# First cross-attention of a two-layer decoder: K and Q projected as three fp32r products of split weights and inputs, and the last unit's division and output projection taken in quarters

## The reference

```python
# x: (4, 512, 256), ctx: (4, 1024, 256), 16 heads of 64
q = x @ Wq; k = ctx @ Wk; v = ctx @ Wv          # fp32, 256 -> 1024 channels
p = softmax(mask(q @ k.T * 0.125))              # a context row that is all zero is masked
x = layernorm(x + (p @ v) @ Wo)
```

## Time and profile before

| | us |
|---|---|
| median of 3 runs (lowest, highest) | 2859.73 (2851.02, 2865.15) |
| the profiled execution, its own time | 2854.95 |
| its span in the trace | 2853.0 |
| `l0_cross` in it | about 267.5 to 1336 |

### The profile page before, as it was taken

The page is one execution under the profiler, slowest core; times in us unless marked ns, Lnnn a source line. Parts: engine busy times, 40 slices in busy tenths (PEclk is TensorE's granted clock), DMA queues, the critical chain, the costliest instruction groups (busy, mean ns, idle before and its releaser), DMA issues.

```text
span 2853.0 us, 37159 instructions
## 1 busy us (share of the span) xinstructions
PE 2618.5 (92%) x14110; PEld 1516.0 (53%) x14110; DVE 1463.5 (51%) x3196; ACT 1096.2 (38%) x1538; POOL 975.4 (34%) x634
## 2 busy tenths in 40 slices
PE   5787999999999999996899999687999999889997
PEld 3343455555555555554566666455434444468886
DVE  3453555555555555553433333366776776355555
ACT  3543344444344444442112111132576666631111
POOL 4675355555555555563100000242121112010001
PEclk8997999999999999997899999888799999789999
DMA  2001000000000000002899999410000000000000
GB/s 102 9 9 49 20 12 32 12 19 12 32 12 19 12 15 22 12 1 84 351 384 378 384 385 383 176 37 18 20 17 17 21 17 9 13 13 23 23 23 32
DMA packets 60192, 228.96 MB, mean 80 GB/s; under 512 B 16536, under 2 KB 30512, under 8 KB 44144
## 3 DMA queue, kind: packets, MB, share of 16 engines
q1 hardware_dynamic: 54128, 209.01, 19.9%
q0 software_dynamic: 3584, 9.84, 1.2%
q10 hardware_dynamic: 2304, 7.75, 0.7%
HBM read 216.73 MB, written 9.70 MB: 79 GB/s over the span
## 4 chain that ended last, share of the span: by engine, by line
PE 75%; ACT 7%; DVE 6%; issue 4%; DMA 4%; POOL 3%; SPq 0%; POOLq 0%; ACTq 0%; DVEq 0%
PE PS L672 8%; PE PS L655 6%; PE PS L702 6%; PE PS L1419 6%; PE PS L2018 6%; PE PS L709 4%; PE PS L1437 4%; PE PS L2006 4%; ACT y_P L1136 4%; DMA m_fb<-in_m_fb 3%; PE PS L1064 3%; PE PS L687 3%; PE PS L1081 3%; PE PS L1047 2%; PE PS L725 2%
## 5 line engine op out<-in xcount | busy, mean ns | idle before, releaser
L890 POOL TENSOR_TENSOR x_A<-x_A,x_P 128x1024 f32<-128x1024 f32 x192 | 453.8, 2364 | 227.1 <-ACT x_P L772 213.2
L825 DVE CUSTOM_DVE_ANT_0 x_junk<-PS,x_mb 128x512 bf16<-128x512 f32 x512 | 331.0, 685 | 348.1 <-PE PS L687 347.8
L1187 DVE TENSOR_REDUCE y_Mx<-PS 128x1 f32<-128x512 f32 x512 | 326.2, 685 | 124.4 <-PE PS L1081 122.5
L772 ACT ACTIVATE x_P<-PS,x_kb 128x1024 f32<-128x1024 f32 x256 | 271.4, 1111 | 222.6 <-PE PS L659 220.7
L1136 ACT ACTIVATE y_P<-PS 128x1024 f32<-128x1024 f32 x256 | 248.5, 1024 | 129.0 <-PE PS L1064 127.4
L1419 PE MATMUL PS<-m_w,m_xt 128*128 128x512 f32 x624 | 283.3, 597 | 0.6 <-issue 0.6
L672 PE MATMUL PS<-x_P,x_V 128*64 128x512 f32 x1024 | 246.1, 602 | 0.0
L655 PE MATMUL PS<-x_Q,x_K 64*128 64x512 f32 x1536 | 228.4, 402 | 0.0
L2018 PE MATMUL PS<-n_xp,n_wp 128*128 128x512 f32 x816 | 210.8, 408 | 4.3 <-POOL n_wp L2134 4.3
L1419 PEld LDWEIGHTS PS<-m_w,m_xt 128*128 128x128 f32 x624 | 116.5, 192 | 116.9 <-issue 115.0
L1640 POOL DMA_INDIRECT m_xb<-xd,m_idxi x39 | 37.1, 950 | 402.3 <-PE PS L1407 369.6
(11 more groups left out here) (312 smaller groups left out, 4079.5 us busy)
## 6 DMA issues: line engine op xcount, KB each, us to landing
m_w<-in_m_w SPq DMA_DIRECT2D x39, 2048.0 KB, 11.3
m_fb<-in_m_fb SPq DMA_DIRECT2D x39, 1024.0 KB, 13.5
m_v<-in_m_w SPq DMA_DIRECT2D x39, 1024.0 KB
x_w<-in_x_w SPq DMA_DIRECT2D x32, 384.0 KB, 3.0
ys<-m_yb SPq DMA_DIRECT2D x39, 128.0 KB
n_wg<-in_n_w SPq DMA_DIRECT2D x17, 256.0 KB, 2.8
x_cT<-in_ctxT SPq DMA_DIRECT2D x4, 1024.0 KB, 5.3
y_c<-in_ctxT SPq DMA_DIRECT2D x6, 512.0 KB, 3.7
```

What stands on the lines that cost most here:

```text
L772: act.e.activation(Pt[gt % 6][:], PS[:, 2 * i:2 * i + 2, :], ACT.Exp, bias=kb[u // 8 % 2][:, kt:kt + 1], scale=scale).then_inc(s["exp"], 1)
L825: dve.e.tensor_tensor_reduce(junk[j % 2][:], ring.bank("max", v, j), mb[b % 2][:, half * 512:half * 512 + 512], 1.0, -3e38, ALU.add, ALU.m ...
L890: pool.e.tensor_tensor(A[u % 2][:], Pt[(gt - 1) % 6][:] if kt == 1 else A[u % 2][:], Pt[gt % 6][:], ALU.add).then_inc(s["add"], 1)
L1187: dve.e.tensor_reduce(Mx[v % 2][:, h, qt, half:half + 1], ring.bank("max", v, j), AX.X, ALU.max).then_inc(s["red"], 1)
```

## The change

1. k and q: the weights of the unit (x_w), the context (x_cT) and the queries (xT) are each split into a high tile rounded to fp32r by ScalarE and a low tile (source minus high) by GpSimd, for unit 0 by VectorE. The step ws splits the weights (128 x 256, one for k and one for q, each unit), cs the context (two of 128 x 1024 a batch) and qs the queries (one of 128 x 1024 a batch). A bank then takes six fp32r products: high x high, high x low, low x high, for two halves of the channels.
2. The split tiles have one buffer each, so a split waits for the last projection that reads the tile. ws of unit u + 3 for k and the first half of cs stand in window t = 2, ws for q, the second half of cs and qs in t = 3; k of unit u + 3 needs them in the window after that. The walk begins one unit earlier (u = -3).
3. For the last unit (31) GpSimd adds up six of the eight key tiles only, and den sums three tiles (x_A and two of x_P) in TensorE. Each quarter's reciprocal is followed at once by its multiplication on VectorE, and wo's half j waits for the quarters up to 2j + 1 in place of the whole mul on GpSimd.
4. To make room, one of the two buffers of x_E, x_R and x_OT, and the other of x_E, are taken from tiles left by the stage before (ax).

```diff
+            W2 = [sbuf(c, f"x_ws{j}", [P, 2, 2, P], F32R) for j in range(2)]
+            C2 = [sbuf(c, f"x_cs{j}", [P, 2, SX], F32R) for j in range(2)]
+            X2 = [sbuf(c, f"x_xs{j}", [P, 2, S], F32R) for j in range(2)]
-            E = [sbuf(c, f"x_E{i}", [P, S]) for i in range(2)]
+            E = [ax["E1"], ax["E0"]]
...
-                2: [("max", 1, 12), ("max", 1, 13), ("q", 2, 0), ("mb", 2, 1), ...
+                2: [("max", 1, 12), ("max", 1, 13), ("q", 2, 0), ("ws", 3, 1), ("cs", 3, 0), ("mb", 2, 1), ...
-                3: [("kb", 2, 0), ...
+                3: [("ws", 3, 0), ("cs", 3, 1), ("qs", 3, 0), ("kb", 2, 0), ...
...
-                return [(u, t) for u in range(-2, n + 3) for t in range(T)]
+                return [(u, t) for u in range(-3, n + 3) for t in range(T)]
...
                         elif name in ("k", "q"):
                             bank = take(pe, name, v, j)
-                            pe.wait_ge(xw[f"w{v % 2}"], 16 * (v // 2 + 1))
-                            pe.wait_ge(xw[f"c{b % 2}"], 16 * (b // 2 + 1))
-                            for kk in range(2):
-                                rhs = cT[b % 2][:, kk, j * 512:(j + 1) * 512] if name == "k" else xT[:, kk, b * S:(b + 1) * S]
-                                m = pe.e.matmul(bank, w[v % 2][:, kk, 1 if name == "k" else 0, :], rhs, start=kk == 0, stop=kk == 1)
+                            pe.wait_ge(s["wl"], 2 * v + (1 if name == "k" else 2))
+                            pe.wait_ge(s["cl"] if name == "k" else s["xl"], 2 * (b + 1) if name == "k" else b + 1)
+                            for i, (p, q) in enumerate(((0, 0), (0, 1), (1, 0))):
+                                for kk in range(2):
+                                    rhs = C2[q][:, kk, j * 512:(j + 1) * 512] if name == "k" else X2[q][:, kk, :]
+                                    m = pe.e.matmul(bank, W2[p][:, kk, 1 if name == "k" else 0, :], rhs,
+                                                    start=i + kk == 0, stop=i + kk == 3)
...
                         elif name == "den":
-                            pe.wait_ge(s["add"], 7 * (v + 1))
-                            for h in range(2):
-                                m = pe.e.matmul(bank[head(h), :], onef[:], A[v % 2][:, h, :], start=True, stop=True)
+                            pe.wait_ge(s["add"], 7 * v + sums(v))
+                            tiles = [A[v % 2]] + [Pt[(8 * v + kt) % 6] for kt in range(sums(v) + 1, 8)]
+                            pe.wait_ge(s["exp"], 8 * v + 8)
+                            for i, src in enumerate(tiles):
+                                for h in range(2):
+                                    m = pe.e.matmul(bank[head(h), :], onef[:], src[:, h, :], start=i == 0, stop=i == len(tiles) - 1)
...
+                        elif name == "ws":
+                            act.wait_ge(xw[f"w{v % 2}"], 16 * (v // 2 + 1))
+                            act.wait_ge(s["proj"], 3 * v - j)
+                            act.e.activation(W2[0][:, :, j, :], w[v % 2][:, :, j, :], ACT.Copy).then_inc(s["wh"], 1)
+                        elif name == "cs":
+                            act.wait_ge(xw[f"c{v // 8 % 2}"], 16 * (v // 16 + 1))
+                            act.wait_ge(s["proj"], 3 * (v - 1) + 2)
+                            act.e.activation(C2[0][:, j, :], cT[v // 8 % 2][:, j, :], ACT.Copy).then_inc(s["ch"], 1)
...
+            def low(e, name, v, j):
...
+                e.wait_ge(s[done + "h"], k)
+                e.e.tensor_tensor(lo, src, hi.bitcast(F32), ALU.subtract).then_inc(s[done + "l"], 1)
...
                             dve.e.reciprocal(r, r).then_inc(s["rec"], 1)
+                            if v == last_u:
+                                dve.wait_ge(s["ev"], v + 1)
+                                dve.wait_ge(s["rec"], 4 * v + j + 1)
+                                dve.wait_ge(s["ob"], 2 * (v // 2 - 1))
+                                dve.e.tensor_tensor(OT[v // 2 % 2][:, v % 2, j * P:(j + 1) * P], E[v % 2][:, j * P:(j + 1) * P], r,
+                                                    ALU.mult).then_inc(s["mulq"], 1)
...
                     for name, v, j in side(u, t):
-                        if name == "mul":
+                        if name in ("ws", "cs", "qs") and v > 0:
+                            low(pool, name, v, j)
+                        elif name == "mul" and v < last_u:
```

More of the change, by code:

```diff
@@ L535, in l0_cross @@
             n, T, NBK, scale = 32, 4, 3, 0.125
-            s = stage_sems(c, 1, "x", "proj hi lo vm vc max red mq turn nm score exp pv add ev den dc rec mul ob res one pad aden adc arec adr arb amul aob ares rt")
+            s = stage_sems(c, 1, "x", "proj hi lo vm vc max red mq turn nm score exp pv add ev den dc rec mul ob res one pad aden adc arec adr arb amul aob ares rt mulq wh wl ch cl xh xl")
             wo = sbuf(c, "x_wo", [P, 8, D])
@@ L544, in l0_cross @@
             A = [sbuf(c, f"x_A{i}", [P, 2, S]) for i in range(2)]
-            E = [sbuf(c, f"x_E{i}", [P, S]) for i in range(2)]
-            R = [sbuf(c, f"x_R{i}", [P, S]) for i in range(2)]
-            OT = [sbuf(c, f"x_OT{i}", [P, 2, S]) for i in range(2)]
+            E = [ax["E1"], ax["E0"]]
+            R = [sbuf(c, "x_R0", [P, S]), ax["R"]]
+            OT = [sbuf(c, "x_OT0", [P, 2, S]), ax["OT"]]
             Mx = [sbuf(c, f"x_Mx{i}", [P, 2, 4, 2]) for i in range(2)]
@@ L584, in side @@
                     v = u + du
-                    first = name in ("ind", "mb", "kb") and v % 8
+                    first = name in ("ind", "mb", "kb", "cs", "qs") and v % 8
                     pair = name in ("wo", "res") and v % 2 == 0
@@ L720, in pe_prog @@
                             pe.wait_ge(xw["wo"], 16)
-                            pe.wait_ge(s["mul"], v + 1)
+                            if v == last_u:
+                                pe.wait_ge(s["mul"], v)
+                                pe.wait_ge(s["mulq"], 2 * j + 2)
+                            else:
+                                pe.wait_ge(s["mul"], v + 1)
                             for i in range(2):
@@ L826, in dve_prog @@
                                                        1.0, -3e38, ALU.add, ALU.max, Mx[v % 2][:, h, qt, half:half + 1]).then_inc(s["red"], 1)
+                        elif name in ("ws", "cs", "qs") and v == 0:
+                            low(dve, name, v, j)
                         elif name == "mq":
```

22 lines of the change are left out of this document (20 added, 2 removed), and 3 rows, old and new, of the table at.

## The result

| | before | after |
|---|---|---|
| median of 5 runs each, side by side (lowest, highest), us | 2857.11 (2851.02, 2865.15) | 2838.70 (2836.60, 2840.94) |
| the profiled execution's span, us | 2853.0 | 2837.0 |

The ratio is 0.9932, with an interval from 0.9913 to 0.9952: the changed kernel is faster by 0.7%, 18.4 us by the medians. The forecast was 2811, 46.3 us less, in a range from 2792 to 2834. The sign is as forecast and the size is two fifths of it; the median lies 4.7 us above the range. A later set of runs on another occasion gave 0.9928 (0.9914 to 0.9942), which agrees.

What follows compares the result with a forecast made beforehand. TensorE's list was taken to bound the steady part; banks 50.7 plus end 6.1 minus batches 6.9 and beginning 3.6 gave 46.3 us saved, forecast 2811 us, own range 2800 to 2822, with rivals 2792 to 2834.

Steps and rivals of the forecast that it cites:

- What bounds the kernel: Steady part, about 300 to 1300 us: TensorE's list sets the length; beginning and end are chains of several engines.
- Rival (1): Steady part: TensorE waits for VectorE to free ring banks, half the gain goes, 25 us instead of 51, 2836; 12%.
- (2): Rival: no waits at the batches, GpSimd overtakes and banks cost 1.28; 61 us gained, 2796; 12%.
- (3): Rival, slower: weight loads not hidden, a bank takes 2.4 us, total 2910; decides from 1.86 us a bank; 3%.
- (4): Rival: no change that can be told, other engines' latency sets the windows' length; around 2855; 3%.
- A bank of k or q: Projections: six fp32r products take 1.365 us instead of 1.91, saving 0.545 a bank, 50.7 us (32 to 59) over 93.
- Its sign for being wrong, a bank above 1.6 us: Profile after: a k or q bank above 1.6 us would show the prediction wrong; 1.3 to 1.45 was expected.
- The splits in the steady part: Added ScalarE copies and GpSimd subtractions, 0.8 and 1.5 us a unit, cost nothing, being covered by TensorE's own list.
- Change of batch: Units 8, 16, 24: first k waits 2.3 us for GpSimd's split context, 6.9 us lost in all (0 to 14).
- a clock below 1.00: Sign of being wrong: TensorE's granted clock below 1.00 in the steady part.
- The beginning: Stage start: splits delay the first k; its first bank ends 4.0 us later, 3.6 us lost (1 to 6).
- The end: Last unit: den follows the values at once, so wo starts 6.1 us earlier; gain 6.1 us (3 to 8).

Runs made afterwards that it cites:

- a3: The changed kernel with q moved in window 2 to directly before the first half of the values; 2831.57 us, 0.9924 of the kernel before.
- a8: The changed kernel with q and both halves of the values one behind the other at the end of window 2; 2819.07 us, 0.9864 of the kernel before.
- b3: The changed kernel with both k parts together, q and both value parts together, and the context split by columns; 2810.69 us, 0.9832 of the kernel before.
- a5: The changed kernel with unit 0's k and q as plain fp32 products from unsplit tiles, subtractions on GpSimd; 2837.33 us, 0.9927 of the kernel before.
- a2: The kernel before with only the last unit's new end, projections still plain fp32; 2852.14 us, 0.9980 of the kernel before.
- a6: The changed kernel with the context split by column halves instead of channel halves; 2826.79 us, 0.9901 of the kernel before.
- b2: The changed kernel with the context split by column halves and q and both value halves side by side; 2819.25 us, 0.9865 of the kernel before.

## Why the prediction missed, step by step

**What bounds the kernel** held. TensorE is busy for 119.35 us of 120 in a steady stretch after, and every ordinary unit became shorter by what its three banks did: 3 x 0.34 is 1.02, measured are 1.0, where the prediction had 1.6. Rival (1), whose 2836 comes near the measured time, is not what happened: it wanted waits in all units, and there are none. Nor are rivals (2), (3) and (4): the waits at the batches came, a bank takes 1.57 and not above 1.86, and the time moved.

**A bank of k or q is the step that failed.** The prediction read two scores' groups of 0.89 and 0.69 us as the price of a change of the kind of product, plain fp32 against fp32r, and concluded that the old bank paid it at its entry and that "the new one should not"; among the candidates it took 1.365 with the words "The row that is the same shape decides". The row was the same in its own products and not in its neighbours. Its sign for being wrong, a bank above 1.6 us, was also set too high to catch this: 1.57 lies between it and the 1.3 to 1.45 that it expected. The 0.20 goes with the part of the array that a group's weights fill. The records of one bank in the trace of after show it, starts in us:

```
543.225  product of L695 (64*128), the last before k
543.546  first weight load of L711 (128*128)
543.548  first product     543.882  second     544.115  third     544.345  fourth
544.799  sixth and last
545.115  first weight load of L731 (128*64), and its product at 545.117
```

Inside the group a product follows the one before by 0.23 us, and its weight load starts beside a product in flight, so it is hidden. At the entry the first load starts 0.321 us after the last product of L695, and the second product follows the first by 0.334; at the exit the next group starts after 0.316. Each of the three intervals is some 0.1 longer than a product. L695 is fp32r as L711 is, so at the entry nothing changes but the shape. So an edge costs up to 0.2 us, about half inside the bank and half in the neighbour, and a bank with two edges takes 6 x 0.2275 + 0.20 = 1.57. The old bank has the same neighbours:

```profile
529.07 0.23 PE PS L687 x2
...
531.22 1.87 PE PS L672 x8
```

It paid the same. Its four records start at 529.235, 529.769, 530.198 and 530.627, and the next group at 531.149: 0.4285 us for a record, 0.106 more at the entry and 0.093 more at the exit. 4 x 0.4285 = 1.71, and 0.20 on top makes its 1.91. The term cancels, and a bank saves 1.71 - 1.365 = 0.345. That is the lower bound that the prediction gave, for a reason that was wrong. In the last stage the alternation is between fp32r and plain fp32 (L2074 and L2062) at one shape, 128*128, and there the records inside a group follow each other by 0.227 to 0.232 us and 12 products take 2.73 in all: the kind of product costs nothing there. This was to be read in the trace of before: the neighbours of the row load 128*128, those of the row don't.

The Trainium skill ("TensorE: Matmul & The Clock Gate", The mechanism) says in one place that weight loads overlap with products in flight only when the group of rows differs, and in another that a load also goes ahead when it targets the background weight buffer. Inside a bank the trace fits the second and not the first: five loads of the same full 128*128 tile start alongside the products before them. Where the shape changes, the first load starts 0.321 us after the last product, 0.09 later than a product of the same shape would have followed.

What the runs show of the cause: the cost is paid per group and not per product (four, six and twelve products), it is paid by old and new banks alike, and each edge taken away gave time back: 0.13 to 0.15 us for q (a3), 0.38 for the two of the second part of the values (a8), 0.22 for the second part of k (from 27.58 to 27.36, b3). That is 0.75 us for four edges, 0.19 in the mean; why they differ is open. The kind of product is cleared by the 0.03 of a8 and by the last stage. That it is the loads which can't be brought forward across such an edge is read from the starts, and no run separates it from something else in the array.

For 93 banks the term is 93 x 0.34 = 31.6 us in place of 50.7, which is 19.1 of the 30.3 us by which the spans missed the forecast. With this term alone put right the forecast would have been 2830, inside the range. The range was also drawn tightly: it ended at 2834, short of rival (1)'s own 2836.

**The splits in the steady part** cost nothing, as said: 0.41 us on ScalarE for 256 columns (0.38 was taken) and 0.73 on GpSimd (0.74).

**Change of batch.** GpSimd's timeline in windows 2 and 3 of unit 5, against the earlier trace rows:

```profile
484.69 4.90 POOL L944 TENSOR_TENSOR x_A<-x_A,x_P 128x1024 f32<-128x1024 f32 x2 [1.91 <-ACT x_P L791]
489.55 0.73 POOL L859 TENSOR_TENSOR x_ws<-x_w,x_ws 128x256 fp32r<-128x256 f32 x1
490.23 2.39 POOL L859 TENSOR_TENSOR x_cs<-x_cT,x_cs 128x1024 fp32r<-128x1024 f32 x1
492.58 1.28 POOL L953 TENSOR_TENSOR x_OT<-ax_E,x_R 128x512 f32<-128x512 f32 x1
493.80 4.90 POOL L944 TENSOR_TENSOR x_A<-x_A,x_P 128x1024 f32<-128x1024 f32 x2
...
499.37 2.35 POOL L859 TENSOR_TENSOR x_cs<-x_cT,x_cs 128x1024 fp32r<-128x1024 f32 x1
```

The order is the one worked out, each duration within 0.1 us. TensorE there, against the earlier trace rows:

```profile
499.48 0.40 PE L695 MATMUL PS<-x_K,x_Q 64*128 64x512 f32 x2
501.86 2.23 PE L711 MATMUL PS<-x_cs,x_ws 128*128 128x512 f32 x6 [1.99 <-POOL x_cs L859]
504.02 2.92 PE L680 MATMUL PS<-x_P,x_V 128*64 128x512 f32 x8
...
509.41 1.65 PE L711 MATMUL PS<-x_cs,x_ws 128*128 128x512 f32 x6
```

The wait is 2.0 in place of 2.3 us, three times. Right behind it, in this place, the clock is low: the bank takes 2.23 and pv (L680) 2.92 us, where 1.64 and 1.94 are usual. Of such stretches the steady part of after has three more than that of before, 4.6 us together. The prediction said only that a clock below 1.00 would make it wrong, and put the term at nothing. With it the steady part closes: 90 of the banks lie between the first turn and the last, 30.6 us; less 3 x 2.3 at the batches (2.0 of waiting and what follows it), 0.9 in units 10, 18 and 26 and 4.6 for the clock that leaves 18.2, and 17.4 are measured. What takes the 0.3 in each of units 10, 18 and 26 is open.

**The beginning**, for the earlier trace rows:

```profile
277.13 1.22 DVE L859 TENSOR_TENSOR x_cs<-x_cT,x_cs 128x1024 fp32r<-128x1024 f32 x1
...
278.49 5.46 PE L711 MATMUL PS<-x_cs,x_ws 128*128 128x512 f32 x12 [5.91 <-DVE x_cs L859]
```

The first k starts 5.2 us later after the last den than before, and 1.7 came back up to the first turn, which I put down to the shorter banks at the low clock. 3.5 lost, 3.6 forecast. TensorE could have begun at 273.3; ScalarE's last copy that k needs ends at 276.87 and VectorE's subtraction at 278.35, so the copies are the longer part. a5 shows that work moved out of this chain comes back behind it.

**The end**, for the earlier trace rows:

```profile
1294.05 3.65 PE L680 MATMUL PS<-x_P,x_V 128*64 128x512 f32 x16
...
1297.53 1.03 PE L731 MATMUL PS<-x_A,x_onef 128*64 128x512 f32 x4
...
1298.39 1.89 PE L731 MATMUL PS<-x_P,x_onef 128*64 128x512 f32 x8
...
1300.32 0.60 ACT L828 ACTIVATE ax_R<-PS 128x512 f32<-128x512 f32 x1 [1.98 <-PE PS L731]
1300.95 0.95 DVE L891 RECIPROCAL ax_R<-ax_R 128x128 f32<-128x128 f32 x1 [10.35 <-ACT ax_R L828]
1302.01 0.29 DVE L896 TENSOR_TENSOR ax_OT<-ax_E,ax_R 128x128 f32<-128x128 f32 x1
...
1303.64 5.41 PE L744 MATMUL PS<-x_wo,ax_OT 128*128 128x256 f32 x16 [3.36 <-DVE ax_OT L896]
```

den begins behind the values, at 1297.53, its 12 records take 2.79 us (2.74 forecast), a quarter takes 0.95 and 0.29 (0.85 and 0.25), and wo starts 6.1 us after den, where it was 7.6 and den stood waiting 4.2. The term of the prediction is the start of wo: it comes 9.3 us after the last exponential in place of 15.2, 5.8 earlier (6.1 forecast), and it is 5.8 in the end alone (a2) too. The last wo is 6.7 earlier in after and 5.5 in a2; the difference is the granted clock while wo runs. In the time the end alone is 0.2%.

**The sum, by spans.** 46.3 were forecast and 16.0 came. Of the 30.3 between them 19.1 are the banks, 4.6 the clock in the steady part, 5.8 the first stage's and 0.8 all the rest. By the medians 18.4 came, and 27.9 are missing: 19.1 for the banks, and 8.8 that the runs don't divide further. The low clock in the steady part is some of it (three stretches more than before in one execution, one in the other, 1.5 to 1.7 us each); whether the rest is the clock elsewhere or chance stays open.

## What to carry to other kernels

A duration that is taken from another stage is only good together with its neighbours: compare what stands before and after the group in both places, not the group alone. When a price is paid by the old form as well as by the new one it drops out of the saving, so write both forms as products plus edges before you subtract; here the old form was at hand with its 1.91 = 4 x 0.4285 + 0.20. And in a written order of small groups it pays to put groups with the same weight shape side by side: three steps moved in a list and a split cut the way it is read took 1% off the changed kernel.

## What the runs showed of the hardware

- An edge between groups whose weights fill different parts of the array costs 0.13 to 0.22 us of TensorE (a3, a8, b3); between fp32r and plain fp32 at the same shape 0 (last stage) to 0.03 us.
- A VectorE instruction with one input in SBUF and one output in bf16 (x_ind, 128 x 2048) takes 1.22 us alone and 2.44 (a6) to 3.18 (b2) beside GpSimd: not only those with two inputs are lengthened.
- With TensorE busy for 99% of a stretch, the granted clock still falls to its lower level for 3.4 us at a time: four times in the steady part of one execution of the changed kernel, twice in another, not at all in a2 and a8, for 1.5 to 1.7 us each.
